# Order of the score, the transposes and the main products in a cross-attention kernel's TensorE queue

## The reference, cut to what matters

```python
q = heads(hidden_states @ W_q)                       # (16, 20, 128, 8)
k_t = heads(text_ehs @ W_k)                          # (16, 20, 124, 8)
v_t = heads(text_ehs @ W_v)
scores_t = jnp.einsum('bhsd,bhtd->bhst', q, k_t) * attn_scale
probs_t = jax.nn.softmax(scores_t, axis=-1)
text_out = jnp.einsum('bhst,bhtd->bhsd', probs_t, v_t)
...
attn_scores = jnp.einsum('bhsd,bhnd->bhsn', q, k_ip) * attn_scale
qsem = _l2norm(jnp.einsum('bhst,bte->bhse', probs_t, text_ehs))
sem = jnp.einsum('bhse,bne->bhsn', qsem, ip_n)
probs_ip = jax.nn.softmax(attn_scores + SEM_SCALE * sem, axis=-1)
probs_ip = probs_ip * spatial_mask[None, None, :, None]
out = text_out + ip_out                              # ip_out = probs_ip @ v_ip
out = out @ W_out + b_out + residual
```

## Time and profile before

| | us |
|---|---|
| median of 3 runs | 226.52 (226.52 to 226.81) |
| profiled execution | 225.47 |
| span of its trace | 223.5 |
| PE busy | 210.6 (94% of the span) |
| DVE busy | 183.7 (82%) |
| ACT busy | 172.7 (77%) |
| POOL busy | 149.3 (67%) |
| granted PE clock, mean | 0.992 |

### The profile page before, as it was taken

How to read it: one execution, slowest core, us unless ns; L and a number is a source line. 1 busy time by engine, 2 the same in 40 slices (tenths; PEclk the granted TensorE clock), 3 DMA queues, 4 the chain that set the end, 5 groups by cost and what they waited for, 6 DMA issues and landing times.

```text
span 223.5 us, 6984 instructions
## 1 busy us (share of the span) xinstructions
PE 210.6 (94%) x1619; PEld 197.6 (88%) x1619; DVE 183.7 (82%) x1147; ACT 172.7 (77%) x569; POOL 149.3 (67%) x255
## 2 busy tenths in 40 slices
PE   8986859999999999999999999999999999998984
PEld 8876749999899999989999999999999999997973
DVE  4726529797988979697979899897979797999893
ACT  2608739897987979788888889697988888897831
POOL 2152301929688696959696977969696969698870
PEclk9996999999999999999999999999999999999999
DMA  5530553555462644565454647264545455461101
GB/s 137 110 121 18 115 148 72 146 142 155 128 164 70 193 112 124 147 158 149 135 155 121 181 103 198 76 181 109 153 123 158 148 144 149 105 167 32 47 1 44
DMA packets 47340, 27.60 MB, mean 123 GB/s; under 512 B 8513, under 2 KB 45538, under 8 KB 47322
## 3 DMA queue, kind: packets, MB, share of 16 engines
q1 hardware_dynamic: 46682, 26.96, 44.8%
q10 hardware_dynamic: 640, 0.43, 0.8%
HBM read 10.14 MB, written 1.52 MB: 52 GB/s over the span
## 4 chain that ended last, share of the span: by engine, by line
PE 68%; DVE 9%; DMA 8%; POOL 4%; issue 4%; ACT 3%; SPq 3%; DVEq 0%; POOLq 0%; ACTq 0%
PE main_ps L952 13%; PE main_ps L954 12%; PE probsT_ps L934 11%; DMA main_rhs<-g_stage 8%; PE pa L924 8%; PE score_ps L984 6%; PE pb L1012 4%; DVE junk L713 3%; PE pb L1024 3%; PE pa L1031 2%; PE main_ps L870 2%; PE pa L1039 2%; POOL rnorm L500 2%; SPq L373 1%; PE probsT_ps L865 1%
## 5 line engine op out<-in xcount | busy, mean ns | idle before, releaser
L612 ACT ACTIVATE probs<-score_ps,negmax 128x124 f32<-128x124 f32 x320 | 93.2, 411 | 1.1 <-DVE negmax L778 1.0
L713 DVE CUSTOM_DVE_ANT_0 junk<-main_ps,probs 128x124 f32<-128x124 f32 x320 | 77.8, 280 | 2.5 <-PE main_ps L954 2.0
L952 PE MATMUL main_ps<-main_rhs,probsT 124*128 124x137 f32 x320 | 64.8, 283 | 2.7 <-DVE small L715 2.7
L954 PE MATMUL main_ps<-main_rhs,probsT 124*128 124x137 f32 x320 | 63.3, 279 | 0.0
L500 POOL TENSOR_TENSOR rnorm<-clamped,exponent 128x20 f32<-128x20 f32 x15 | 53.2, 3544 | 1.2 <-DVE clamped L698 1.2
L778 DVE TENSOR_REDUCE negmax<-score_ps 128x4 f32<-128x496 f32 x80 | 53.1, 663 | 0.0
L952 PEld LDWEIGHTS main_ps<-main_rhs,probsT 124*128 124x128 f32 x320 | 48.9, 190 | 4.5 <-ACT probsT L565 2.0
L565 ACT ACTIVATE probsT<-probsT_ps 124x512 f32<-124x512 f32 x80 | 50.9, 636 | 2.5 <-PE probsT_ps L934 1.7
L934 PE MATMUL probsT_ps<-ident_sb,probs 128*124 128x128 f32 x320 | 49.0, 276 | 0.0
L954 PEld LDWEIGHTS main_ps<-main_rhs,probsT 124*128 124x128 f32 x320 | 48.7, 188 | 0.0
L934 PEld LDWEIGHTS probsT_ps<-ident_sb,probs 128*124 128x124 f32 x320 | 39.1, 141 | 5.3 <-issue 0.4
(11 more groups left out here) (165 smaller groups left out, 343.5 us busy)
## 6 DMA issues: line engine op xcount, KB each, us to landing
main_rhs<-g_stage SPq DMA_DIRECT2D x16, 660.0 KB, 4.2
vrep<-vip_d SPq DMA_DIRECT2D x13, 320.0 KB, 3.6
k_diag<-k_stack SPq DMA_DIRECT2D x60, 64.0 KB, 2.2
ctxT_sb<-ctxT SPq DMA_DIRECT2D x16, 124.0 KB, 2.7
xT_sb<-xT SPq DMA_DIRECT2D x16, 80.0 KB, 2.1
xn_sb<-xn SPq DMA_DIRECT2D x15, 80.0 KB, 2.0
out<-out_sb SPq DMA_DIRECT2D x15, 80.0 KB, 1.7
k_diag<-k_stack SPq DMA_DIRECT2D x60, 16.0 KB, 1.8
```

Source lines behind the costliest of these rows:

```text
L612: last = act.activation(probs[p][:, h, :], score_ps[(p * G + g) % 2][:, j * TOK:j * TOK + T], ACT.Exp, bias=negmax[p][:, h:h + 1])
L713: dve.tensor_tensor_reduce(junk[:, 2 * r + a, :], u, probs[wb][:, h, :], 1.0, 0.0, ALU.mult, ALU.add, norm2[wb][:, h:h + 1])
L952: pe.matmul(main_ps[r][:, 0:MAIN], probsT[mp][:, 2 * r, :], blk[:, RW - MAIN:RW], start=True, stop=True)
L954: pe.matmul(main_ps[r][:, MAIN:2 * MAIN], probsT[mp][:, 2 * r + 1, :], blk[:, 0:MAIN], start=True, stop=True).then_inc(s_main, 1)
```

## The change

In `window` of PE's program the call of `transposes` moves from behind the score (and, in step 4, behind L1001 and L1002) to behind `mains`. In step 3 it thereby also passes the output projection L1012. The order of a step is then: score, L1001 and L1002 in step 4, L1012 in step 3, main products of group grp - 3, transposes of group grp - 2, and the rest. No instruction is added or taken away, no wait is changed, and the other engines' programs and the part from L1064 on stay as they are.

```diff
@@ -1001,8 +1001,6 @@
                         pe.matmul(pb[:, 0:TOK], stacked(k_split, G - 1), ident_r_sb[:, :], start=True, stop=True)
                         pe.matmul(pb[:, TOK:TOK + S], stacked(q_split, G - 1), ident_r_sb[:, :], start=True,
                                   stop=True).then_inc(s_kq4, 1)
-                    if has_group(w, g, 2):
-                        transposes(b, p, g)
                     if g == 3 and has(w, lag=3):
 
                         if w == 3:
@@ -1013,6 +1011,8 @@
                         mm.then_inc(s_final_mm, 1)
                     if has_group(w, g, 3):
                         mains(b, p, i, g, w)
+                    if has_group(w, g, 2):
+                        transposes(b, p, g)
                     if g == 0 and has(w, ahead=1):
 
                         if w == 0:
```

## The result

The changed kernel takes 252.19 us (median of 4 runs, 250.43 to 253.03), the one before 226.56 (226.52 to 226.81) beside it. The ratio is 1.111, with a 95% interval of 1.106 to 1.116: slower by 25.6 us, where 22.2 was forecast. The profiled execution is one of 253.03 us with a span of 251.0; before it was 225.47 with 223.5.

A forecast was written before the change was run, and what follows sets the result against it. PE bounds the kernel, its matmuls back to back, so each added wait counts in full. Sum 16.7 + 2.8 + 2.7 = 22.2 us more, against the median 226.52: 248.7 us, range 239 to 259.

The forecast's parts named there:

- The round trip: PE transposes to ACT's copy to PE's main products: 1.46 us in sum, ends 1.29 and 1.58.
- the return: From the end of ACT's copy to the start of PE's main product: taken as 0.07 us.
- The stretch of the first product: First main product behind a wait stretched from 0.40 to 0.47 us; 0.05 taken into the round trip.
- The transposes' own slot: PE time of a group's transposes, taken as 0.44 us and subtracted from the round trip to get each step's stall.
- windows 3 to 14: 12 windows at 1.47 us of stalls, 17.6, less 0.9 of PE's waits for DVE now covered: 16.7 us more.
- Window 15 and the turn: From window 14's step 4 main products to L1070's: 14.92 us in place of 12.17, 2.7 more.
- Windows 0 to 2: Start of the run: window 0's DMA wait covers all, windows 1 and 2 stall, together 2.8 us more.
- the second rival: PE's clock falls because PE stands in every step; one half-clock stretch per window gives 274 us; chance 0.05.
- Step 0 at nothing: No stall in step 0, since `project_gkv` alone is the larger part of 1.43 us of filler.
- ACT late (the first): Copy and exponentials share ACT's queue; margins of 0.4 us in steps 0, 1, 4 used up: 261 us; chance 0.12.
- Headroom (the third): PE isn't full; 0.46 us of each window's stall vanishes in gaps the weight loads show: 242 us; chance 0.06.
- Faster or equal (the fourth and fifth): Fourth: earlier main products remove DVE waits, 223.6 us, chance 0.04. Fifth: stalls and shorter waits cancel, nothing measurable, chance 0.03.

The follow-up runs named there:

- the other profiled execution of the changed kernel: The changed kernel run once more, unaltered, as a base for the last runs: 251.45 us, ratio 1.114 to the kernel before.
- the run with step 0 alone: The kernel before, with the transposes moved behind the main products in step 0 only: 232.44 us, ratio 1.023.

## Why the prediction was right, and what it sized wrong

**What bounds the kernel** was right: PE's queue was full, no work was added, and the waits came in full. Steps and windows say so, and so does the run with only the output projection moved.

**The round trip.** Forecast 1.46 us with 0.05 of stretch in it, so 1.41 from start to start; measured 1.46 to 1.47. Transposes to copy were 0.72 as taken, the copy 0.60 (0.62 taken). The term that was mis-sized is the return: 0.14, where I took 0.07, near the lower of two rows of DVE's (0.05 and 0.15). The upper was the right one in the loop, the lower in the windows written out, in steps where the copy ends last. The stretch of the first product was mis-sized too: the second starts 0.34 us behind it (117.69 to 118.03), where it is 0.24 elsewhere, so 0.10 and not 0.05. Together 0.10 more in each of steps 1, 2 and 4.

**The transposes' own slot.** I took 0.44, from a place where they stand ahead of the main products. Ahead of the score, which leaves one record, it is 0.36 (124.54 to 124.90), and so ahead of the turnings of k and q. The main products had this place before, at 0.85 (118.92 to 119.77), and have 0.94 now. That is 0.08 more stall in steps 2 and 4, and 0.08 less in step 3, where the transposes themselves are the cost. With both corrections the forecast of each step is 0.34, 0.44, 0.36 and 0.71; measured are 0.37, 0.44, 0.36 and 0.68.

**The sum.** For windows 3 to 14 the forecast was 16.7 and the measured difference 20.1. It is 12 times 1.86 = 22.3, less 2.2. Of these, 1.5 are there because the average window of before is 12.23 us, not 12.10 (I had 0.9), and 0.7 because windows 3 and 14 are written out and have the shorter circle, which I left out. Window 15 and the turn: 2.4 measured, 2.7 forecast. Windows 0 to 2: 5.0 measured, 2.8 forecast; here the second rival came true once. In 35.5 to 41.0 the clock was granted at 0.69, between its levels of 1.2 and 2.4 GHz, behind this wait:

```profile
35.29 0.47 PE L952 MATMUL main_ps<-main_rhs,probsT 124*128 124x137 f32 x2 [2.25 <-DVE small L715]
...
38.21 0.66 PE L952 MATMUL main_ps<-main_rhs,probsT 124*128 124x137 f32 x2
```

The four main products take 1.78 us there in place of 0.94 (38.21 to 39.99). Before, the wait at this place was 1.84 us and the clock stayed at 1.00. But in the other profiled execution of the changed kernel the wait was 2.25 too and the clock 1.00 in 36.0 to 41.0, so the wait alone doesn't decide it. From these main products to the score of step 3 it is 5.54 us in the one (35.29 to 40.83) and 4.17 in the other (35.04 to 39.21): the slow stretch took about 1.4 us. In the other execution windows 0 to 2 are 3.2 us longer than before, near the forecast; the rest is a part of the spread and not of the mechanism.

**Step 0 at nothing** was right in the changed kernel (2.15 and 2.14) and wrong by its reason. I argued that its filler is long enough; the run with step 0 alone lost 5.9 us with no wait on PE in that step. What I left out is the queue behind the copy: a late copy makes `q_split` late, DVE waits for it, and `oT` behind. In the changed kernel PE is late itself by then, and this lateness seems to lie beneath its stalls; no run shows that by itself. That I cost ACT's and DVE's side at nothing was right for the sum alone.

**The rivals.** ACT late (the first): no; ACT idles ahead of 76 of 80 copies. The clock (the second): once, not in mid-kernel, where it is 1.00. Headroom (the third): PE's weight loads had left 0.46 us of the window free. For PE the Trainium skill (Perfetto Trace Analysis, "Identifying the Most-Contended Engine") judges headroom by the busy share of the weight loads, beside the share of peak arithmetic, and not by that of the matmuls. Nothing of the stalls vanished in these 0.46 us: each window grew by 1.86 us, not by 1.01. Taken as room that absorbs a stall, as the third rival did, this measure does not agree with the trace; the distances of the starts did tell. Faster or equal (the fourth and fifth): the circle would have had to be at or under 1.02 to 1.2 us; it is 1.29 even without the loop.

**Signs.** The windows were forecast at 13.5 to 13.6 us and are 13.96, by the terms above.

What stays open: what in the loop lengthens the circle and why turned waits lengthen it outside the loop, why the DMA of `g_stage` is late more often in the kernel before written out, and the 2 us of step 1 moved alone. None of the versions is faster than the kernel before.

## What to carry to other kernels

When one queue is full, put between a producer and the reader of its product as much ready work as the whole round trip through the other engine takes, here 1.46 us and not only the 0.60 of the copy; an order that is ready earlier for the reader is worth nothing if it takes that work away. Count the round trip from start to start, with the return from rows of the same loop, and the cover that a moved instruction gave to others on its way (the transposes covered two). And ask not only what the queue itself waits for, but what stands behind the late item on the engine that serves it: the bill can come three steps later. Read such effects from the steady windows: a median can hide two that cancel.

## What the runs showed of the hardware

- A round trip PE, ACT, PE took 1.46 us in the hardware loop and 1.29 written out, of which 0.60 is the copy of 124x512. The order of the two semaphore waits mattered: turned, it took 0.21 us from a window in the loop and made the circle outside the loop 1.44 us where it was 1.29.
- Four fp32 transposes take PE 0.44 us ahead of an fp32 product with two records and 0.36 ahead of one with one record; four main products take 0.94 ahead of the transposes (115.28 to 116.22) and 0.85 ahead of the turning of k (118.92 to 119.77 before). The first product behind a wait is followed by the next after 0.34 us, later ones after 0.24.
- Waits for two semaphores were put down to DVE 30 times with 15.0 us; shorter norms made that 9.2 and left the window in the loop at 13.96, since the copy came last. The distance from the end of each candidate to the start decides, not the name in the list.
- PE took its matmuls in order: the transposes, ready since their exponentials, started at 127.03, only behind the main products that were held until 126.00. The Trainium skill (TensorE: Matmul & The Clock Gate, "Step-by-step: what each phase is for") says that matmuls stay in program order and only weight loads are pulled ahead. For the matmuls the trace agrees; the load at 125.99 waited for the same copy as its product, so this place doesn't show a load pulled ahead.
